# A two-layer attention and mixture-of-experts kernel: first context group loaded in four column pieces, setup block folded into the values stage

## The chip, the cores and the metric

The kernel runs on one core of one Trainium2 chip. The metric is device time of one execution in microseconds (us), lower is better. One execution is also taken by the hardware profiler; its rows are in microseconds from the first instruction of the span, unless marked ns. About 0.5% is what a measurement of this kernel can tell from no change.

## The reference

Inputs are `x` and `ctx_2048`, both 16 x 128 x 512 in float32 (16 batches of 128 rows), and the weights of four blocks, each added to `x`: an mLSTM attention whose keys and values are the context, a feed-forward block with 8 routed experts and a shared one, a cross attention of 16 heads with rms-normed queries and keys, and a linear layer with ternary weights. What matters here is the very first work of the program, which belongs to the third block but depends on the context alone:

```python
v_img = (img_ctx @ vi_w + vi_b).reshape(B, -1, H, D)     # 2048 x 512 times 512 x 2048
```

The context is also turned (rows to columns) for the keys and for the gates of the first block, so the same stage makes the turned context, its two-part split for the three-pass products, and the gates.

## The kernel before, in words

All work is written out per engine in blocks; each block ends with a barrier of all engines, and inside a block engines meet through semaphores only.

`setup` (line 158) is a block of its own, with work on GpSimd alone: four memsets (identity, two epsilons, ones), then an `affine_select` (L171) that makes the identity matrix for TensorE's transposes. Then comes `mlstm`, whose first block is the values stage, `values_and_gates` (line 185).

The values stage computes the values of one context tile of 128 rows (a "unit", 52 of them in all) times 512 weight columns (a "quad" of four heads). The contraction of 512 is cut in four chunks of 128. The context comes in four groups of four batches (1 MB each, `load_ctx`, L249), and a group and chunk together are one turn `t` = 4 x group + chunk:

- TensorE `turn(t)` (L585): four 128x128 transposes (L593) into one bank. For group 0 it waits for the whole group; from t = 4 on it waits as well until DVE and ACT have read the same bank, which is `trail_done` and `plain_done` at t - 3.
- ACT `turn_lead(t)` (L386) rounds the bank into `lead`; DVE `turn_trail(t)` (L480) writes bank minus lead into `trail`; ACT `turn_plain(t)` (L393) copies the bank once more and stores it to memory (L395).
- the weight's chunk c gets the same split: ACT `wl` (L406), DVE `wt` (L485).
- TensorE `first_chunk(c)` (L611): 12 products (three passes, four tiles) of chunk c for units 0 to 3, in banks 0 to 3. Later units (L597) do their 12 products in one go, each after ACT or DVE has emptied its bank (`keep_even` L400, `keep_odd` L534).

Each engine runs its list in the order written. ACT's opening order is lead 0, wl 0, lead 1, wl 1, lead 2, wl 2, lead 3, wl 3; plain 0 to 3; lead 4 to 7; plain 4, plain 5; keep_even 0, keep_even 2; plain 6, plain 7; then per unit. DVE's is trail 0, wt 0, ... trail 3, wt 3; trail 4 to 7; keep_odd 1 and 3; then per unit, among it the next weight's `wt` from unit 10 on and row statistics from unit 8 on. TensorE's is turns 0 to 3, first_chunk 0, turn 4, first_chunk 1, turn 5, first_chunk 2, turns 6 and 7, first_chunk 3; then for each unit from 4 on a turn (while there are any) and the unit.

SyncE's queue: group 0 (1 MB, rows of 2 KB), the four weight chunks (256 KB each, L260), group 1; after turn 3 group 2; after turn 7 group 3, the eight small loads of gate weights and biases (L269 to L273), the store of the first values (L283), two of x (L254) and the next weight quad of 1 MB (L290), which GpSimd splits (L370).

```python
            for t in range(C):
                turn(t)
            for c in range(C):
                first_chunk(c)
                if c < C - 1:
                    turn(C + c)
                if c == C - 2:
                    turn(C + c + 1)
```

Of the kernel before, what the change touches and what calls it, by code (L numbers as in the profile page):

```python
# [20 lines left out]
ALU = mybir.AluOpType  # L21
# [3 lines left out]
P = 128  # L25
B, S, D = 16, 128, 512
T = B * S
C = D // P
GB = 4
# [44 lines left out]
class Phase:  # L74
# [23 lines left out]
    def sb(self, name, shape, dt=F32):  # L98
        return self.stack.enter_context(self.nc.sbuf_tensor(f"{self.name}_{name}", shape, dt))

    def sem(self, name):
        self.sems.append(self.nc.alloc_semaphore(name=f"{self.name}_{name}"))
        return self.sems[-1]
# [51 lines left out]

def setup(nc, K):

    with Phase(nc, "setup") as ph:  # L160
        blank, made = ph.sem("blank"), ph.sem("made")
        block = ph.block()

        @block.gpsimd
        def _(pool):
            nc.gpsimd.memset(K.ident[:], 0.0).then_inc(blank, 1)
            nc.gpsimd.memset(K.eps5[:], 1e-5)
            nc.gpsimd.memset(K.eps6[:], 1e-6)
            nc.gpsimd.memset(K.ones[:], 1.0).then_inc(blank, 1)
            pool.wait_ge(blank, 2)  # L170
            nc.gpsimd.affine_select(out=K.ident[:], in_=K.ident[:], compare_op=ALU.not_equal, fill=1.0,  # L171
                                    base=0, pattern=[[-1, P]], channel_multiplier=1).then_inc(made, 1)
            pool.wait_ge(made, 1)

# [8 lines left out]
def values_and_gates(nc, K, M, A, E1, x_split, lead, trail, keep, a, v_dram, tail_dram, split_dram, xn_dram, ct_dram, g_dram):  # L185
    with Phase(nc, "values") as ph:
        sb, sem = ph.sb, ph.sem
# [13 lines left out]
        stage = [A.kT[:].rearrange("p c n -> p (c n)").rearrange("p (b d) -> p b d", b=GB), A.ctx[:]]  # L201
# [5 lines left out]
        out = [sb("out", [P, 4, GB, DH1]), A.out]  # L207
# [20 lines left out]
        turned, lead_done, trail_done, plain_done = sem("turned"), sem("lead_done"), sem("trail_done"), sem("plain_done")  # L228
        wl_done, wt_done = sem("wl_done"), sem("wt_done")
        product, even_done, odd_done = sem("product"), sem("even_done"), sem("odd_done")  # L230
        cleared, masks = sem("cleared"), sem("masks")
        wsum_done, wc_lead, wc_trail = sem("wsum_done"), sem("wc_lead"), sem("wc_trail")
        xn_done, x_turned, xT_done = sem("xn_done"), sem("x_turned"), sem("xT_done")
# [7 lines left out]
        block = ph.block()  # L241
        ps = K.ps

        def bank(t):
            return 4 + t % 4

        @block.sync
        def _(sp):
            def load_ctx(g):  # L249
                sp.dma_start(stage[g % 2], a["ctx_2048"][g * GB:(g + 1) * GB].rearrange("b s d -> s b d")  # L250
                             ).then_inc(ctx_loaded[g], 16)
# [3 lines left out]
                             ).then_inc(x_loaded[g], 16)  # L255

            w_dram = a["L1_xattn_vi_w"]
            load_ctx(0)
            for c in range(C):
                sp.dma_start(raw[:, c, :], w_dram[c * P:(c + 1) * P, 0:N]).then_inc(first_loaded[c], 16)  # L260
            load_ctx(1)
            sp.wait_ge(turned, C)
# [23 lines left out]
            for u in range(UNITS):  # L286
# [11 lines left out]
                if u in SPLITS:  # L298
                    g = SPLITS[u]
# [54 lines left out]
        @block.gpsimd  # L354
        def _(pool):
            own = Own(pool, own_pool)
            nc.gpsimd.memset(w_gate[:], 0.0)
            nc.gpsimd.memset(bias[:], 0.0).then_inc(cleared, 1)
            nc.gpsimd.memset(keep[:], 1.0)
            own(nc.gpsimd.memset(pen[:], 0.0))  # L360
            nc.gpsimd.memset(keep[:, :, 0:1], 0.0)
            nc.gpsimd.memset(pen[:, :, 0:1], -FAR).then_inc(masks, 1)
            for q in range(1, QUADS):
                pool.wait_ge(raw_loaded, 16 * q)
                if q > 1:
                    pool.wait_ge(product, OPENS[q - 1])
                if q == TAIL[0] + 2:
                    pool.wait_ge(tail_stored, 32)
                for c in range(C):
                    nc.gpsimd.tensor_scalar(wl[:, q % 2, c, :], raw[:, c, :], 1.0, None, ALU.mult).then_inc(wl_done, 1)  # L370
            Phase.clear_over(nc)
# [212 lines left out]
        def _(pe):  # L584
            def turn(t):  # L585
                g, c = divmod(t, C)
                if c == 0:
                    pe.wait_ge(ctx_loaded[g], 16)
                if t >= C:
                    pe.wait_ge(trail_done, t - C + 1)  # L590
                    pe.wait_ge(plain_done, t - C + 1)
                for b in range(GB):
                    ins = nc.tensor.transpose(ps[:, bank(t), b * S:(b + 1) * S], stage[g % 2][:, b, c * P:(c + 1) * P],  # L593
                                              K.ident[:])
                ins.then_inc(turned, 1)
# [68 lines left out]
                                                  row[:, b * S:(b + 1) * S], K.ident[0:32, 0:32])  # L664
                    ins.then_inc(nat_T, 1)

            for t in range(C):
                turn(t)
            for c in range(C):
                first_chunk(c)  # L670
                if c < C - 1:
                    turn(C + c)
                if c == C - 2:
                    turn(C + c + 1)
            for u in range(GB, UNITS):
                if u + C < G * C:
                    turn(u + C)
# [2607 lines left out]
def two_layers(nc, a, out):  # L3285
# [20 lines left out]
    with ExitStack() as stack:  # L3306
        kept = lambda name, shape: stack.enter_context(nc.sbuf_tensor(name, shape, F32))
        K = Kept()
# [8 lines left out]
        R.slot = stack.enter_context(nc.sbuf_tensor("slot", [P, 2, B], U32))  # L3317
        R.expert = stack.enter_context(nc.sbuf_tensor("expert", [P, TILES + 1], U32))
        K.stats, K.mv, K.rstd = kept("stats", [P, B, 6]), kept("mv", [P, B, 2]), kept("rstd", [P, B])
        setup(nc, K)  # L3320
        routed_weights = [a[f"L0_ffn_w_{n}"] for n in ("gate", "up", "down")]
        with Phase(nc, "of_ffn") as outer:
            with Phase(nc, "of_shared") as inner:
# [44 lines left out]
```

## Time and profile before

| | |
|---|---|
| runs | 1348.18, 1343.0, 1348.6 us; median 1348.18 |
| profiled execution | 1345.04 us, of it span 1343.3 us, granted TensorE clock 0.987 |
| busy share of the span | PE 95%, PEld 79%, DVE 63%, ACT 55%, POOL 28% |
| DMA | 277.06 MB, mean 206 GB/s |
| TensorE idle before its first transpose | 7.85 us |

PE is TensorE's matmuls and transposes, PEld its weight loads, DVE VectorE, ACT ScalarE, POOL GpSimd, SP SyncE; SPq and ACTq are their sequencers issuing DMAs. A row of the timeline gives the start, the duration, the engine, the line, the operation, output and inputs, and in brackets how long the engine had been idle before and what released it. Rows with xN merge N instructions that follow each other. Matmuls are pipelined, so the distance between two starts tells more than a duration.

### The profile page before, as it was taken

What the parts mean: (1) busy time and instruction counts of PE and PEld (TensorE: products, weight loads), DVE (VectorE), ACT (ScalarE), POOL (GpSimd) and SP (SyncE); (2) the same over time, 40 slices, a digit from 0 to 9 for tenths busy, and PEclk for the clock granted to TensorE, in tenths of its full rate; (3) what the DMA queues carried; (4) which work ended last, traced back from release to release, by engine and by line L of the source; (5) the groups of instructions that cost most, each with busy time, mean ns of one, the idle gap of its engine ahead of it and who ended that gap; (6) DMA issues with size and microseconds to landing.
All of it is one profiled execution on the core that took longest, in us unless ns stands there. A gap on an engine that the chain in (4) does not pass through costs nothing. (4 is left out here: it accounts for less than half of the span.)

```text
span 1343.3 us, 24403 instructions
## 1 busy us (share of the span) xinstructions
PE 1279.5 (95%) x7358; PEld 1059.4 (79%) x7359; DVE 841.2 (63%) x1613; ACT 741.6 (55%) x1831; POOL 379.5 (28%) x353
## 2 busy tenths in 40 slices
PE   7999997999999899899999989999989999999998
PEld 6787776777777778688877778878888888888986
DVE  3545546778779863644445477553577777777865
ACT  5225538787886431454455445445775655565561
POOL 0111014274737016399131342144010000000041
PEclk9999999999999899899999999999989999999999
DMA  7897399787864394666559776564475555555403
GB/s 255 290 365 255 139 317 322 268 265 253 280 223 166 88 345 174 223 180 208 148 170 314 255 261 189 158 210 172 143 213 166 160 157 167 159 162 157 120 28 126
DMA packets 166599, 277.06 MB, mean 206 GB/s; under 512 B 29744, under 2 KB 58160, under 8 KB 166256
## 3 DMA queue, kind: packets, MB, share of 16 engines
q1 hardware_dynamic: 140704, 220.50, 51.2%
q0 software_dynamic: 8672, 29.37, 6.7%
q10 hardware_dynamic: 17136, 26.09, 5.3%
q8 instruction: 47, 0.77, 0.2%
q14 instruction: 40, 0.33, 0.1%
HBM read 167.11 MB, written 108.80 MB: 205 GB/s over the span
## 5 line engine op out<-in xcount | busy, mean ns | idle before, releaser
L120 PE MATMUL banks<-of_shared_split,key_lead 128*128 128x512 f32 x256 | 104.7, 409 | 11.5 <-DVE key_trail L1403 10.1
L2984 ACT ACTIVATE prob<-banks,attend_row,rq 128x128 f32<-128x128 f32 x248 | 110.5, 470 | 0.0
L2997 ACT ACTIVATE attend_ol<-banks,of_attend_vbias 128x512 fp32r<-128x512 f32 x64 | 44.2, 691 | 117.0 <-PE banks L3196 117.0
L120 PE MATMUL banks<-wo,attend_ol 128*128 (+1 forms) x256 | 106.2, 415 | 0.0
L120 PE MATMUL banks<-queries_rows_split,queries_wl 128*128 128x512 f32 x256 | 100.8, 394 | 0.0
L122 PE MATMUL banks<-wo,attend_ot 128*128 (+1 forms) x256 | 100.7, 393 | 0.0
L122 PE MATMUL banks<-of_shared_split,key_trail 128*128 128x512 f32 x256 | 100.6, 393 | 0.0
L121 PE MATMUL banks<-of_shared_split,key_lead 128*128 128x512 f32 x256 | 100.1, 391 | 0.0
L121 PE MATMUL banks<-wo,attend_ol 128*128 (+1 forms) x256 | 99.9, 390 | 0.0
L122 PE MATMUL banks<-queries_rows_split,queries_wt 128*128 128x512 f32 x256 | 99.8, 390 | 0.0
L121 PE MATMUL banks<-queries_rows_split,queries_wl 128*128 128x512 f32 x256 | 99.7, 390 | 0.0
L2966 POOL TENSOR_TENSOR x_kept<-x_kept,attend_tern_bias 128x512 f32<-128x512 f32 x12 | 15.5, 1294 | 282.6 <-ACT of_attend_raw L3023 281.0
L2634 DVE TENSOR_TENSOR queries_total<-queries_total,queries_sq 128x512 f32<-128x512 f32 x60 | 45.0, 751 | 75.2 <-ACT queries_sq L2547 75.2
L2543 ACT ACTIVATE queries_head<-banks,queries_bias 128x512 f32<-128x512 f32 x64 | 44.1, 689 | 81.7 <-PE banks L122 76.1
L1013 ACT ACTIVATE heads_dec<-mlstm_gmax,mlstm_nat 128x128 f32<-128x128 f32 x256 | 81.3, 389 | 10.0 <-POOL mlstm_gmax L921 4.8
L120 PE MATMUL banks<-of_shared_split,of_ctx_lead 128*128 128x512 f32 x208 | 84.0, 404 | 2.0 <-DVE of_ctx_trail L480 1.8
L1198 DVE TENSOR_TENSOR heads_total<-heads_total,heads_ksq 128x512 f32<-128x512 f32 x60 | 56.6, 943 | 42.1 <-ACT heads_ksq L1055 41.8
L122 PE MATMUL banks<-of_shared_split,of_ctx_trail 128*128 128x512 f32 x208 | 82.3, 396 | 0.0
L3085 DVE TENSOR_TENSOR x_kept<-x_kept,banks 128x512 f32 (+1 forms) x64 | 44.0, 688 | 60.8 <-PE banks L122 60.2
L121 PE MATMUL banks<-of_shared_split,of_ctx_lead 128*128 128x512 f32 x208 | 81.7, 393 | 0.0
L3177 PEld LDWEIGHTS banks<-attend_kn,q_ahead 128*128 128x128 f32 x496 | 66.0, 195 | 6.2 <-issue 1.9
L120 PEld LDWEIGHTS banks<-of_shared_split,key_lead 128*128 128x128 f32 x256 | 48.1, 188 | 28.5 <-DVE key_trail L1403 14.9
(399 smaller groups left out, 3535.0 us busy)
## 6 DMA issues: line engine op xcount, KB each, us to landing
mlstm_gmax<-running_max SPq DMA_DIRECT2D x32, 512.0 KB, 6.2
k_heads<-heads_key ACTq DMA_DIRECT2D x64, 256.0 KB, 4.4
q_heads<-queries_head SPq DMA_DIRECT2D x64, 256.0 KB, 2.6
q_ahead<-q_heads SPq DMA_DIRECT2D x64, 256.0 KB, 4.2
of_attend_k<-k_heads SPq DMA_DIRECT2D x60, 256.0 KB, 4.1
of_attend_v<-v_heads SPq DMA_DIRECT2D x60, 256.0 KB, 3.2
key_raw<-in_L_xattn_ki_w SPq DMA_DIRECT2D x20, 512.0 KB, 5.5
sorted_rows<-of_shared_split SPq DMA_DIRECT2D x2, 5120.0 KB, 27.6
```

The costliest lines, as they stand in the source:

```text
L120: nc.tensor.matmul(out, lead_l, lead_r, start=first, stop=False)
L121: nc.tensor.matmul(out, lead_l, trail_r, start=False, stop=False)
L122: return nc.tensor.matmul(out, trail_l, lead_r, start=False, stop=last)
L1013: ins = nc.scalar.activation(dec[:, n % 2, b], gmax[:, h // 2 % 4, h % 2 * N + b * S:h % 2 * N + (b + 1) * S], ACT.Exp, scale=-1.0, bias=M ...
L1198: nc.vector.tensor_tensor(t, t, ksq[:, m % 2, :], ALU.add).then_inc(total_done, 1)
L2543: nc.scalar.activation(head[:, u % HEADS_RING, :], ps[:, u % 4, :], ACT.Identity, bias=bias[:, h:h + 1]).then_inc(head_done, 1)
L2634: nc.vector.tensor_tensor(t, t, sq[:, u % 2, :], ALU.add).then_inc(total_done, 1)
L2966: nc.gpsimd.tensor_tensor(K.x[:, b, :], K.x[:, b, :], tern_bias[:], ALU.add).then_inc(tern_bias_done, 1)
L2984: ins = nc.scalar.activation(prob[:, j % 2, b, :], ps[:, j % 2, b * S:(b + 1) * S], ACT.Exp, bias=row[:, j % 2, 1, b:b + 1], scale=rq[:, b ...
L2997: nc.scalar.activation(ol[:, par, j, :], ps[:, 4 + j % 2, :], ACT.Identity, bias=vbias[:, bass.ds(quad_of(it) * 4 + j, 1)]).then_inc(ol_do ...
L3085: nc.vector.tensor_tensor(xb, xb, ps[:, 6 + b % 2, :], ALU.add).then_inc(acc_done, 1)
L3177: ins = nc.tensor.matmul(ps[:, j % 2, s], q[:, j, s], kn[:, j % 2, s], start=True, stop=True)
```

## The change

The setup block goes; its instructions stand at the head of GpSimd's list in the values stage, with one semaphore (`made`) that TensorE waits for before its first transpose. Group 0 of the context is loaded in four pieces of 128 columns (256 KB each, runs of 512 bytes), each ahead of the weight chunk of the same number, with a semaphore each. TensorE's order becomes turns 0 and 1, first_chunk 0, turn 2, first_chunk 1, turn 3, first_chunk 2, turns 4 to 7, first_chunk 3. The lists of ACT and DVE stay as they are.

```diff
-def setup(nc, K):
-
-    with Phase(nc, "setup") as ph:
-        blank, made = ph.sem("blank"), ph.sem("made")
-        block = ph.block()
-
-        @block.gpsimd
-        def _(pool):
...
+def setup(nc, K, pool, blank, made):
+    nc.gpsimd.memset(K.ident[:], 0.0).then_inc(blank, 1)
+    nc.gpsimd.memset(K.ones[:], 1.0)
+    nc.gpsimd.memset(K.eps5[:], 1e-5)
+    nc.gpsimd.memset(K.eps6[:], 1e-6)
+    pool.wait_ge(blank, 1)
+    nc.gpsimd.affine_select(out=K.ident[:], in_=K.ident[:], compare_op=ALU.not_equal, fill=1.0,
+                            base=0, pattern=[[-1, P]], channel_multiplier=1).then_inc(made, 1)
...
             w_dram = a["L1_xattn_vi_w"]
-            load_ctx(0)
             for c in range(C):
+                sp.dma_start(stage[0][:, :, c * P:(c + 1) * P],
+                             a["ctx_2048"][0:GB, :, c * P:(c + 1) * P].rearrange("b s d -> s b d")).then_inc(ctx_first[c], 16)
                 sp.dma_start(raw[:, c, :], w_dram[c * P:(c + 1) * P, 0:N]).then_inc(first_loaded[c], 16)
             load_ctx(1)
...
         def _(pool):
             own = Own(pool, own_pool)
+            setup(nc, K, pool, blank, made)
             nc.gpsimd.memset(w_gate[:], 0.0)
...
                 g, c = divmod(t, C)
-                if c == 0:
+                if g == 0:
+                    pe.wait_ge(ctx_first[c], 16)
+                elif c == 0:
                     pe.wait_ge(ctx_loaded[g], 16)
...
-            for t in range(C):
-                turn(t)
+            pe.wait_ge(made, 1)
+            turn(0)
+            turn(1)
             for c in range(C):
                 first_chunk(c)
-                if c < C - 1:
-                    turn(C + c)
+                if c + 2 < C:
+                    turn(c + 2)
                 if c == C - 2:
-                    turn(C + c + 1)
+                    for t in range(C, 2 * C):
+                        turn(t)
...
-        setup(nc, K)
```

## Rows read from the trace of the kernel before

**Rows 1.** The page: busy time, share of the span, instructions of TensorE

```profile
PE 1279.5 (95%) x7358; PEld 1059.4 (79%) x7359; DVE 841.2 (63%) x1613; ACT 741.6 (55%) x1831; POOL 379.5 (28%) x353
```

**Rows 2.** Timeline of all engines from the start: start, duration, engine, line, operation

```profile
0.81 0.20 POOL L166 MEMSET ident<- 128x128 f32 x1 [0.29 <-POOLq L3359]
...
1.47 0.28 POOL L171 TENSOR_SCALAR_AFFINE_SELECT ident<-ident 128x128 f32<-128x128 f32 x1 [0.24 <-POOL ones L169]
2.22 0.45 SPq L250 DMA_DIRECT2D mlstm_kT<-in_ctx  x1
...
2.73 2.24 SPq L260 DMA_DIRECT2D mlstm_gmax<-in_L_xattn_vi_w  x4
...
7.85 3.66 PE L593 MATMUL banks<-ident,mlstm_kT 128*128 128x128 f32 x16 [7.85 <-DMA mlstm_kT<-in_ctx]
```

**Rows 3.** Windows of the opening: stretch, length, granted clock, DMA share, GB/s

```profile
3.80:4.20 0.40, 1.00 0.07 26
...
5.00:6.00 1.00, 1.00 1.03 401
```

**Rows 4.** DMA issues of the whole span: size of one, median us to landing

```profile
of_ffn_raw<-sorted_rows SPq DMA_DIRECT2D x39, 256.0 KB, 3.0
```

**Rows 5.** Timeline of DVE: split of the first weight chunk

```profile
10.24 0.68 DVE L485 TENSOR_TENSOR of_shared_split<-mlstm_gmax,of_shared_split 128x512 fp32r<-128x512 f32 x1
```

**Rows 6.** Timeline of TensorE alone: first chunks of units 0 to 3, unit 4

```profile
11.18 0.56 PE L120 MATMUL banks<-of_shared_split,of_ctx_lead 128*128 128x512 f32 x1
...
14.11 0.60 PE L593 MATMUL banks<-ident,mlstm_ctx 128*128 128x128 f32 x4
14.47 0.47 PE L120 MATMUL banks<-of_shared_split,of_ctx_lead 128*128 128x512 f32 x1
...
20.48 1.03 PE L593 MATMUL banks<-ident,mlstm_ctx 128*128 128x128 f32 x8
21.28 0.48 PE L120 MATMUL banks<-of_shared_split,of_ctx_lead 128*128 128x512 f32 x1
...
24.90 0.47 PE L120 MATMUL banks<-of_shared_split,of_ctx_lead 128*128 128x512 f32 x1 [0.17 <-ACT of_ffn_raw L400]
```

**Rows 7.** Timeline of ACT: leads, copies kept for the store, first eviction

```profile
9.00 0.60 ACT L386 ACTIVATE of_ctx_lead<-banks 128x512 fp32r<-128x512 f32 x1 [5.49 <-PE banks L593]
...
13.01 0.61 ACT L393 ACTIVATE mlstm_gmax<-banks 128x512 f32<-128x512 f32 x1
...
17.06 0.60 ACT L386 ACTIVATE of_ctx_lead<-banks 128x512 fp32r<-128x512 f32 x1 [0.40 <-ACT mlstm_gmax L393]
...
21.12 1.09 ACT L386 ACTIVATE of_ctx_lead<-banks 128x512 fp32r<-128x512 f32 x2 [2.59 <-PE banks L593]
22.09 0.61 ACT L393 ACTIVATE mlstm_gmax<-banks 128x512 f32<-128x512 f32 x1
...
24.16 1.08 ACT L400 ACTIVATE of_ffn_raw<-banks 128x512 f32<-128x512 f32 x2 [0.40 <-ACT mlstm_gmax L393]
```

**Rows 8.** Timeline of SyncE's queue: what follows turn 7

```profile
21.55 0.37 SPq L250 DMA_DIRECT2D mlstm_ctx<-in_ctx  x1
...
30.31 0.40 SPq L283 DMA_DIRECT2D v_heads<-of_ffn_raw  x1
...
33.92 1.05 SPq L290 DMA_DIRECT2D mlstm_gmax<-in_L_xattn_vi_w  x1
```

**Rows 9.** Timeline of all engines about unit 12

```profile
47.57 5.87 POOL L370 TENSOR_SCALAR of_shared_split<-mlstm_gmax 128x512 fp32r<-128x512 f32 x4 [43.48 <-DMA mlstm_gmax<-in_L_xattn_vi_w]
...
51.31 0.67 DVE L480 TENSOR_TENSOR of_ctx_trail<-banks,of_ctx_lead 128x512 fp32r<-128x512 f32 x1
...
52.04 0.58 PE L120 MATMUL banks<-of_shared_split,of_ctx_lead 128*128 128x512 f32 x1 [1.82 <-DVE of_ctx_trail L480]
...
55.79 0.39 PE L120 MATMUL banks<-of_shared_split,of_ctx_lead 128*128 128x512 f32 x1
```

**Rows 10.** Windows after that wait: PE busy, granted clock, DMA share, GB/s

```profile
54.00:56.00 2.00, 2.00 (x6) 0.57 1.05 406
```

More of the change, by code:

```diff
@@ L154, in root @@
                                   ).then_inc(self.rooted, 1)
-def setup(nc, K):
-    with Phase(nc, "setup") as ph:
-        blank, made = ph.sem("blank"), ph.sem("made")
-        block = ph.block()
-        @block.gpsimd
-        def _(pool):
[L166 to L173, printed above, removed]
+def setup(nc, K, pool, blank, made):
[6 more added lines that the diff above has]
+                            base=0, pattern=[[-1, P]], channel_multiplier=1).then_inc(made, 1)
 class Gates:
@@ L230, in values_and_gates @@
         product, even_done, odd_done = sem("product"), sem("even_done"), sem("odd_done")
+        blank, made = sem("blank"), sem("made")
+        ctx_first = [sem(f"ctx_first{c}") for c in range(C)]
         cleared, masks = sem("cleared"), sem("masks")
```

## The prediction

> **What bounds the kernel now.** I read the page first: TensorE is busy 95% of the span [rows 1], so a change can gain only where TensorE stands still or runs at its lower clock, and an earlier start is kept only if nothing further on gives it back. Then the timeline of the opening. GpSimd enters the setup block at 0.81, the identity is made at 1.47, SyncE issues the first load only at 2.22, and the first transpose starts at 7.85, released by that load [rows 2]. The first product follows at 11.18 [rows 6], with the split of the first weight chunk on DVE (10.24) just ahead of it [rows 5]. From there to unit 4 at 24.90 TensorE runs without a hole but for 0.17 us [rows 6]. The next hole is 1.82 us before unit 12 at 52.04 [rows 9]. Its chain: the next weight quad is issued at 33.92 [rows 8] and lands at 47.57; GpSimd splits its chunks; DVE, which takes its list in order, needs the first of them for a `wt`, then does statistics, and only then at 51.31 the trail that unit 12 needs [rows 9]. That load's place is set by SyncE: group 3 goes out at 21.55, after turn 7, then eight small loads until 30.31, then three of 1 MB and this one [rows 8]. After the hole the clock is low, 0.57 of full over 54 to 56 us [rows 10], which is the 1.2 GHz level for most of it.
>
> **The barrier.** Without the block SyncE issues at 0.81 instead of 2.22, the time at which GpSimd enters the first block against the second [rows 2]: 1.41 us earlier. GpSimd's five instructions now run beside the load. The identity is ready at about 1.8 (1.47 + 0.28), far ahead of any landing, so the new wait on `made` costs 0; if the cover were gone it would cost its 0.9 us. The memsets behind it on GpSimd move to about 1.8 and nobody waits for them before turn 7. ACT's table load also moves ahead.
>
> **The first piece.** No row shows a piece of 256 KB in runs of 512 bytes as the first load. From below: 256 KB lands in 3.0 us at the median [rows 4]. From above: the whole 1 MB took 5.63 us (2.22 to 7.85) [rows 2]. I build it: 1.98 us from issue to data (still 26 GB/s at 3.80 to 4.20, so data starts at 4.20), 0.26 MB at 401 GB/s is 0.66 us [rows 3], and a tail. The tail of the 1 MB load: 1.05 MB at the same rate is 2.62, so its data ends near 6.82 and the transpose starts 1.03 later. Sum 3.67 us; turn 0 at 4.48. Between turn 0 and the first product I keep 3.33 us (7.85 to 11.18), since ACT and DVE do the same four steps: first product at 7.81, **3.37 us earlier**. Bounds: 0.81 + 3.0 + 3.33 = 7.14 (4.04 earlier) and 0.81 + 5.63 + 3.33 = 9.77 (1.41 earlier). The issues: five DMAs took 2.22 to 4.97 [rows 2], 0.55 each, so nine end near 5.8; group 1 is issued some 0.7 us later than now (4 x 0.55 = 2.2 more, less 1.41) and is needed by turn 4 only at about 17. Weight chunk 0 goes out second and comes some 0.7 us after the piece, while ACT wants it 1.65 us after turn 0: hidden. Half the rate for the short runs would add 0.66, inside the bounds.
>
> The Trainium skill speaks against small pieces (DMA: Bandwidth & Descriptors, Rules for kernel authors: at least 1 MiB per DMA for full bandwidth) and gives a fixed cost of about 2.0 us per DMA; by an estimate from that page the piece would land after about 2.7 us and the first product would come 1.0 us earlier than in my sum. The traces' 3.0 us for 256 KB agrees only roughly.
>
> **The order on TensorE and ACT.** Here something is given back. Call the start of the first product F. First_chunk 0 takes 2.93 (11.18 to 14.11), a turn 0.36 (14.11 to 14.47), a later chunk 2.83 (from 14.47 to 20.48 are two and a turn) [rows 6]. Turn 3 now stands behind two chunks and turn 2: F + 6.12. ACT's lead 3 follows 0.64 later (20.48 to 21.12), wl 3 and plain 0 follow at 0.50 each (four pairs from 9.00 to 13.01), so plain 0 is at F + 7.76 and, four copies with their stores taking 4.05 (13.01 to 17.06), plain 3 at F + 10.80 and lead 4 at F + 11.81 [rows 7]. Turn 7 wants plain 3; from an ACT start to TensorE's go is 0.74 (24.16 to 24.90), so turn 7 starts at F + 11.54 and first_chunk 3 at F + 11.90. Now they start at F + 9.70 (20.48 + 0.40) and F + 10.10 (21.28): **1.84 and 1.80 us are given back**, 0.72 of it the two turns moved behind F, the rest waiting. And ACT is late for more: four leads from F + 11.81 on, 0.485 each (two in 0.97, 21.12 to 22.09), plain 4 at F + 13.75, keep_even 0 2.07 later (22.09 to 24.16) at F + 15.82, unit 4 at F + 16.56. Now it is F + 13.72: 2.84 given back, with a new hole of about 1.5 us before unit 4, since first_chunk 3 and turn 8 end at F + 11.90 + 2.83 + 0.36 = F + 15.09.
>
> **Unit 12.** SyncE's list from group 3 on follows turn 7, so the weight quad, and with it unit 12, moves by 3.37 - 1.84 = 1.53 us earlier. TensorE's own way there moves by only 3.37 - 2.84 = 0.53, so the hole shrinks from 1.82 to 0.82 and unit 12 still follows SyncE's chain. DMA is full there (406 GB/s at share 1.05 [rows 10]) and I take its bytes as unchanged.
>
> **The clock.** The 16 first transposes take 3.33 us, 0.21 each [rows 2, 6], eight later ones 0.80 us, 0.10 each [rows 6]: the first run at half speed, 1.2 GHz by this reading, though the granted clock reads 1.00 [rows 3], and the products at 11.18 already run fast. In the changed kernel only eight transposes, with a gap, come before first_chunk 0. What a slow stretch costs is at unit 12: nine products from 52.04 to 55.79 take 3.75 us [rows 9] against 9 x 0.236 = 2.12 at the pace above: 1.63 us. First_chunk 0 loses between 0 and 1.63; I take 1.63, as its row is the nearest, a product stretch after a hole. At unit 12 the other way: after a hole of 0.82 us instead of 1.82 the clock may hold, which gives 0 to 1.63 back; I take 1.63, as the nearer row is the 0.17 us hole at 24.90 with no fall behind it. The Trainium skill (TensorE: Matmul & The Clock Gate, Part 1) says that the default state is throttled and that activity releases it; by that the first product starts slow, as in my sum, and without it the sum would be 1.63 better.
>
> **The sum.** 3.37 - 1.84 - 1.63 + 1.63 = 1.53 us faster, 1343.5 on the profiled execution's 1345.04. That execution lies 3.1 us under the median of 1348.18, and the runs spread over 5.6 us; the mean of all four times is 1346.2, and I take the forecast from there: **1344.7 us**. Best bound 4.04 - 1.84 + 1.63 = 3.8 faster; worst 1.41 - 1.84 - 1.63 = 2.1 slower, where unit 12's clock falls as now.
>
> **Rivals.**
> - The opening's gain arrives whole. If copies on ACT are not the brake that I count (1.84 more), or first_chunk 0 runs fast (1.63 more), or both, 3.2 to 5.0 us are gained: about 1342. For it: rows 6 show TensorE nearly without holes. Against it: turn 7 does wait for plain 3 in the code, and ACT's start times are read, not guessed.
> - Slower: ACT's lateness wins. The mechanism is the wait of turn 7 for plain 3, 1.84 us, plus the slow first_chunk 0, 1.63 us, against the earlier start. It decides from the point where turn 0 starts later than 4.38 us (3.47 lost against 3.47 won) and no clock is regained at unit 12; at 6.44 it ends 2.1 us slower: 1348.3. For it: my 4.48 sits right at that point. Against it: the smaller hole at unit 12. By the same page of the skill the new hole before unit 4 could also lower the clock, another 1.63 there; this eats the hole at unit 12 and changes the end by about 1.
> - The change does not do what it says: SyncE still starts at 2.22, as entering the block costs the same. Then 3.37 - 1.41 - 1.84 = 0.12 gained: 1346.1.
> - Something outside the first 60 us moves by several us, by the scatter that the runs show.
>
> **How the numbers follow.** Forecast 0.50, gain whole 0.22, slower 0.17, no earlier start 0.05, outside 0.06. The range takes both bounds from 1346.2 (1342.4 and 1348.3) and half the spread, 2.8: 1339.6 to 1351. Half a per cent, which is what a measurement here can tell, is 6.7 us; no case but the last reaches that alone, the second with favourable scatter. So faster by over 0.5% 0.08, within 0.89, slower 0.03.
>
> **What would show it.** SyncE's first issue at 0.8, first transpose at 4.5, first product at 7.8 with its chunk taking 4.6 instead of 2.93; TensorE idle before turns 6 and 7 with ACT L393 as the releaser, and about 1.5 us before unit 4, which starts at 7.81 + 16.56 + 1.63 = 26.0, released by ACT L400; unit 12 at 52.04 - 1.53 + 1.63 = 52.1, with a hole under 1 us and the clock up after it. I am wrong in mechanism if turn 7 does not wait for ACT, or if the first product is not earlier by at least 1.4 us; wrong in size if the whole moves by over 6.7 us.

## The result and the profile after

The changed kernel takes **1350.91 us** (median of 20 runs, 1345.29 to 1359.12), the kernel before, run on the same chip, 1346.22 us (20 runs, 1341.01 to 1351.64). The ratio is 1.0033, 95% interval 1.0017 to 1.0048: slower by 4.7 us. That lies inside the half per cent that counts as no change and just inside the stated range, but on the other side from the 1.5 us gain that I forecast.

The profiled execution took 1347.16 us (span 1345.4). On the page TensorE's share still reads 95%, so this line says nothing about a change of a third of a per cent:

```profile
PE 1283.9 (95%) x7358; PEld 1062.1 (79%) x7359; DVE 839.6 (62%) x1613; ACT 742.0 (55%) x1831; POOL 376.9 (28%) x353
```

SyncE's queue, from its timeline (start, duration, engine, line, operation), beside [rows 2, 8]:

```profile
0.81 0.45 SPq L253 DMA_DIRECT2D mlstm_kT<-in_ctx  x1
1.32 0.49 SPq L255 DMA_DIRECT2D mlstm_gmax<-in_L_xattn_vi_w  x1
...
4.93 0.43 SPq L244 DMA_DIRECT2D mlstm_ctx<-in_ctx  x1
16.27 0.38 SPq L244 DMA_DIRECT2D mlstm_kT<-in_ctx  x1
21.72 0.37 SPq L244 DMA_DIRECT2D mlstm_ctx<-in_ctx  x1
22.13 2.18 SPq L264 DMA_DIRECT2D values_w_gate<-in_L_xattn_Wi  x3
24.35 4.96 SPq L264 DMA_DIRECT2D values_w_gate<-in_L_xattn_Wf  x3
29.35 1.43 SPq L267 DMA_DIRECT2D values_bias<-in_L_xattn_bi  x1
...
33.65 1.11 SPq L285 DMA_DIRECT2D mlstm_gmax<-in_L_xattn_vi_w  x1
```

The first issue is at 0.81 as forecast. The line to look at is the one at 16.27: the load of context group 2, which waits for turn 3. My prediction speaks of groups 1 and 3 and never of this one.

TensorE's timeline, against [rows 2, 6]; in brackets the idle time before an instruction and what ended it:

```profile
3.96 1.08 PE L591 MATMUL banks<-ident,mlstm_kT 128*128 128x128 f32 x4 [3.96 <-DMA mlstm_kT<-in_ctx]
6.22 1.12 PE L591 MATMUL banks<-ident,mlstm_kT 128*128 128x128 f32 x4 [1.18 <-DMA mlstm_kT<-in_ctx]
7.14 0.76 PE L120 MATMUL banks<-of_shared_split,of_ctx_lead 128*128 128x512 f32 x1
7.71 0.63 PE L121 MATMUL banks<-of_shared_split,of_ctx_lead 128*128 128x512 f32 x1
8.13 0.63 PE L122 MATMUL banks<-of_shared_split,of_ctx_trail 128*128 128x512 f32 x1
...
12.40 0.64 PE L591 MATMUL banks<-ident,mlstm_kT 128*128 128x128 f32 x4
...
15.64 0.60 PE L591 MATMUL banks<-ident,mlstm_kT 128*128 128x128 f32 x4
...
20.06 0.63 PE L591 MATMUL banks<-ident,mlstm_ctx 128*128 128x128 f32 x4 [0.18 <-ACT mlstm_gmax L389]
21.06 0.63 PE L591 MATMUL banks<-ident,mlstm_ctx 128*128 128x128 f32 x4 [0.37 <-ACT mlstm_gmax L389]
...
26.07 0.47 PE L120 MATMUL banks<-of_shared_split,of_ctx_lead 128*128 128x512 f32 x1 [1.20 <-ACT of_ffn_raw L396]
```

The first product comes 4.04 us earlier than before (7.14 against 11.18), but its chunk takes 5.26 us (7.14 to 12.40) instead of 2.93, because the products start 0.43 apart instead of 0.23 in this profile. Turn 3 is at 15.64. Turns 6 and 7 wait for ACT's copies, unit 4 waits for its eviction, and so unit 4 starts 1.17 us *later* than before. ACT itself, in its timeline, stands idle for 4.58 and 2.09 us before leads 2 and 3; that is where the copies of turns 0 to 2 would have had room:

```profile
13.07 0.60 ACT L382 ACTIVATE of_ctx_lead<-banks 128x512 fp32r<-128x512 f32 x1 [4.58 <-PE banks L591]
...
16.28 0.60 ACT L382 ACTIVATE of_ctx_lead<-banks 128x512 fp32r<-128x512 f32 x1 [2.09 <-PE banks L591]
...
17.29 0.59 ACT L389 ACTIVATE mlstm_gmax<-banks 128x512 f32<-128x512 f32 x1
```

Windows of the kernel before (stretch, length, busy time and count on PE, PEld, DVE, ACT, POOL, then granted clock, DMA share, GB/s):

```profile
12.00:18.00 6.00, 6.00 (x32) 4.95 (x32) 2.83 (x6) 4.08 (x9) 0.00 (x0) 1.00 0.97 367
18.00:24.00 6.00, 6.00 (x32) 5.04 (x31) 2.96 (x5) 2.71 (x5) 0.00 (x0) 1.00 0.26 82
```

and of the changed one:

```profile
12.00:18.00 6.00, 6.00 (x31) 4.89 (x30) 2.38 (x4) 2.72 (x5) 0.00 (x0) 1.00 0.06 19
18.00:24.00 6.00, 5.45 (x32) 4.41 (x31) 2.25 (x5) 4.35 (x8) 0.00 (x0) 1.00 0.99 331
```

Before, the DMA engines work from 12 to 18 us (2.2 MB) and rest from 18 to 24 (0.5 MB), so the list that follows turn 7 finds them free. Now it is the reverse: 0.1 MB, then 2.0 MB. Group 2 (out at 16.27 instead of 11.54) and the four stores of the turned context (from 17.91 on instead of 13.65) have slid into the stretch in which group 3 and the eight small loads go out.

In this execution that did no harm yet. The weight quad lands at 47.24 (47.57 before), and unit 12 starts at 51.71 with a short hole and the granted clock stays at 1.00, as forecast [rows 9, 10]; timeline of all engines:

```profile
47.24 5.88 POOL L366 TENSOR_SCALAR of_shared_split<-mlstm_gmax 128x512 fp32r<-128x512 f32 x4 [43.86 <-DMA mlstm_gmax<-in_L_xattn_vi_w]
...
51.71 0.50 PE L120 MATMUL banks<-of_shared_split,of_ctx_lead 128*128 128x512 f32 x1 [0.31 <-DVE of_ctx_trail L476]
```

It is also one of the quicker executions of the changed kernel, 3.75 us under the median, so one trace can't settle this case; further profiles of both kernels stand below.

### The profile page after: what moved, and what is told of

The parts are those of the page before. It is cut to its first block and busy times, and to the rows that moved or that the text cites. A ratio compares the mean times of both kernels' runs of the same rounds, so it can differ in the third digit from the quotient of the medians.

```text
span 1345.4 us, 24387 instructions
## 1 busy us (share of the span) xinstructions
PE 1283.9 (95%) x7358; PEld 1062.1 (79%) x7359; DVE 839.6 (62%) x1613; ACT 742.0 (55%) x1831; POOL 376.9 (28%) x353
## 5 line engine op out<-in xcount | busy, mean ns | idle before, releaser
L120 PE MATMUL banks<-of_shared_split,key_lead 128*128 128x512 f32 x256 | 106.2, 415 | 8.8 <-DVE key_trail L1403 8.4
L121 PE MATMUL banks<-of_shared_split,key_lead 128*128 128x512 f32 x256 | 102.1, 399 | 0.0
```

Source lines behind the costliest of these rows:

```text
L120: nc.tensor.matmul(out, lead_l, lead_r, start=first, stop=False)
L121: nc.tensor.matmul(out, lead_l, trail_r, start=False, stop=False)
```

## The experiments

The expectations are quoted as they were written before each run, and they name theories. Theory A: the difference is chance, from stretches at the lower clock that fall now here, now there. Theory B: the pieces or the new order on TensorE bring the loss. Theory C: losing the barrier brings it. Theory D, which grew out of the first four runs: the new order sends group 2 out late, and the list behind it makes the next weight quad late. Ratios are to the kernel before, measured on the same chip, with 95% intervals.

**The parts by themselves.** `e1_barrier_only` folds the constants into the stage and keeps the whole load and the old order:

```
-        setup(nc, K)
...
+            setup(nc, K, pool, blank, made)
...
+            pe.wait_ge(made, 1)
```

> Setup block folded into the values stage, loads and TensorE order as before. Theory A (the opening is worth what it shows and the 4.7 us come from extra stretches at the lower clock between 190 and 320 us that either kernel can get by chance): TensorE's stream is 1.4 us ahead from the first transpose to 448 us, the number of low-clock stretches before 448 us varies from one to three, the time is within 2 us of before. Theory B (the pieces or the new order on TensorE bring the loss): 1.4 us faster, with one low-clock stretch before 448 us as before. Theory C (losing the barrier brings it, by what it does to later stages): 3 us or more slower.

Measured: 1347.64 us, ratio 1.0010 [0.9987, 1.0033]. First transpose at 6.42 instead of 7.85, first product at 9.71, group 2 out at 10.09, quad landed at 46.90, unit 12 at 51.37. The barrier's 1.4 us arrive at TensorE, half of them is left at unit 12, and the end shows no gain.

`e2_pieces_only` is the changed kernel with the block of its own put back (the reverse of that diff).

> Four pieces and the new TensorE order, setup block kept. Everything of the opening as in the changed kernel but 1.4 us later: first transpose at 5.4, hole before unit 4 of 1.2 us, TensorE 0.6 us ahead of before at 60 us. Theory A: time within 2 us of before. Theory B: slower than before by 4 to 6 us. Theory C: within 1 us of before.

Measured: 1349.47 us, 1.0029 [1.0012, 1.0046]. A loss is there without the barrier's removal, so the pieces or the order bring one; at 3.0 us it is smaller than the 4 to 6 expected. Group 2 goes out at 16.75, the quad lands at 51.62.

`e3_act_fill` uses ACT's idle time before leads 2 and 3:

```
-            for t in range(C):
-                turn_plain(t)
+                if c == 1:
+                    turn_plain(0)
+                    turn_plain(1)
+                if c == 2:
+                    turn_plain(2)
+            turn_plain(3)
```

> The changed kernel, with ACT's copies plain 0 and 1 moved ahead of lead 2 and plain 2 ahead of lead 3, into the 4.6 us in which ACT stands idle. The holes before turns 6 and 7 (0.18 and 0.37) and before unit 4 (1.20) go; if TensorE's way to unit 12 were the limit the gain would be 1.7, but unit 12 hangs on the load that SyncE issues after turn 7, which comes 0.6 to 0.9 us earlier, so that much is gained and a hole of up to 1.5 us stands before unit 12 again. Theory A: between 1 faster and 2 slower than the changed kernel by chance of the clock. Theory that the delay on ACT is what costs the 4.7 us: back to before or faster.

Measured: 1349.36 us, 1.0024 [1.0005, 1.0043]. The holes before turns 6 and 7 are gone and the one before unit 4 shrinks to 0.3 us, yet the time is still lost. Its quad lands at 46.31, earlier than in any profile of the kernel before. Waiting for ACT is real, but taking it away does not win the time back.

**The same kernels again**, without an edit: `e4_changed_again`, `e13_changed_third`, `e14_changed_fourth`, `e18_changed_same_chip`, and of before `e5_before_again`, `e15_before_third`.

> The changed kernel once more, for a second profile of it. Theory A: the opening to 60 us is the same within 0.3 us, the low-clock stretches between 60 and 448 us stand at other places or in another number, and the time is 3 to 6 us over before again if the loss is real. If the stretches stand at the same three places (193, 224, 309) they belong to the kernel, not to chance.

> The kernel before, once more, for a second profile of it. Theory D (turn 3 is late in the changed kernel, so group 2 and the four stores of the turned context go out 4.3 to 4.7 us later and run into group 3 and the eight small loads; the queue behind them, with the next weight quad, lands late and unit 12 waits): the next weight quad is split by GpSimd from 47.6 again, within 0.5 us, unit 12 starts at 52.0. Theory A (chance of the clock): unit 12 moves by some us from profile to profile in this kernel too.

> A third profile of the changed kernel. If the loss sits before unit 12 (theory D), unit 12 starts later than 52.0 in most profiles of it: 51.7 and 56.7 so far, so 53 to 57 here. If it sits elsewhere (theory A), 51.5 to 52.

> A fourth profile, same expectations: theory D 53 to 57 for the start of unit 12, theory A 51.5 to 52.

> A third profile of the kernel before. Theory D: unit 12 at 52 to 53 again (52.04 and 52.9 so far), the issue of the small loads over at 30 to 31.3. Theory A: as far spread as the changed kernel's.

> The changed kernel beside it on the same chip, for the comparison: 1350 to 1351, unit 12 between 51.7 and 56.7.

The changed kernel came out at 1350.88 us, 1.0027 [1.0002, 1.0052], and 1349.38 us, 1.0015 [0.9998, 1.0032] (e18), with single executions of 1346.33 and 1349.49 (e13, e14); before at 1346.99, 1.0001 [0.9978, 1.0024], and a single 1346.95 (e15). The difference repeats, though it is smaller and not clear of noise in e18. Their profiles show where they part (the last column is the DMA share over 32 to 34 us):

| profile | group 3 out | small loads through | quad landed | from group 3 | unit 12 | hole before it | DMA share |
|---|---|---|---|---|---|---|---|
| before | 21.55 | 30.20 | 47.57 | 26.0 | 52.04 | 1.8 | 1.05 |
| before, e5 | 21.89 | 31.20 | 48.13 | 26.2 | 52.60 | 2.0 | 0.97 |
| before, e15 | 21.90 | 30.49 | 48.08 | 26.2 | 52.55 | 2.0 | 1.07 |
| changed | 21.72 | 31.25 | 47.24 | 25.5 | 51.71 | 0.3 | 0.95 |
| changed, e18 | 21.54 | 30.95 | 47.05 | 25.5 | 51.52 | 0.3 | 1.06 |
| changed, e14 | 21.40 | 32.45 | 49.08 | 27.7 | 53.55 | 2.5 | 0.51 |
| changed, e13 | 21.50 | 32.35 | 49.53 | 28.0 | 54.00 | 2.8 | 0.63 |
| changed, e4 | 21.27 | 33.06 | 50.63 | 29.4 | 55.09 | 4.1 | 0.31 |

The kernel before needs 26.0 to 26.2 us from group 3's issue to the quad's landing every time. The changed one needs 25.5 to 29.4, and within its five profiles the landing is late where SyncE was late in getting through the small loads: up to 31.3 it lands at about 47, past 32.3 at 49 and later. In the late ones, and only there, the DMA engines are partly idle over 32 to 34 us. Its latest profile, e4, in the timelines of SyncE, GpSimd and TensorE:

```profile
15.82 0.38 SPq L244 DMA_DIRECT2D mlstm_kT<-in_ctx  x1
21.27 0.37 SPq L244 DMA_DIRECT2D mlstm_ctx<-in_ctx  x1
21.68 2.36 SPq L264 DMA_DIRECT2D values_w_gate<-in_L_xattn_Wi  x3
24.08 5.62 SPq L264 DMA_DIRECT2D values_w_gate<-in_L_xattn_Wf  x3
29.75 2.82 SPq L267 DMA_DIRECT2D values_bias<-in_L_xattn_bi  x1
...
35.33 1.45 SPq L285 DMA_DIRECT2D mlstm_gmax<-in_L_xattn_vi_w  x1
...
50.63 1.50 POOL L366 TENSOR_SCALAR of_shared_split<-mlstm_gmax 128x512 fp32r<-128x512 f32 x1 [47.24 <-DMA mlstm_gmax<-in_L_xattn_vi_w]
...
55.09 0.50 PE L120 MATMUL banks<-of_shared_split,of_ctx_lead 128*128 128x512 f32 x1 [4.08 <-DVE of_ctx_trail L476]
```

and its windows:

```profile
12.00:18.00 6.00, 6.00 (x32) 5.03 (x31) 2.58 (x4) 2.86 (x6) 0.00 (x0) 1.00 0.24 46
...
32.00:34.00 2.00, 2.00 (x12) 1.65 (x11) 1.08 (x2) 0.96 (x2) 0.00 (x0) 1.00 0.31 87
```

against the kernel before:

```profile
32.00:34.00 2.00, 2.00 (x10) 1.63 (x10) 0.69 (x1) 0.67 (x2) 0.00 (x0) 1.00 1.05 382
```

A load of one bias takes SyncE 2.82 us to issue. The small loads hold SyncE until 33.06, and the DMA engines run dry while it is held and just after: share 0.31 over 32 to 34 us, where before has 1.05. The big loads that should feed them stand behind the small ones. e2, e16 and e17, whose quads land late as well, show such a gap too: 0.61 over 32 to 34 in e2, 0.39 over 30 to 31 in e16, 0.50 over 34 to 36 in e17. Why one bias load can hold SyncE so long no run shows.

**Moving loads only.** The opening on TensorE and ACT is the changed kernel's in both of these. `e6_changed_small_early` puts the small loads behind group 1:

```
             load_ctx(1)
-            sp.wait_ge(turned, C)
-            load_ctx(2)
-            sp.wait_ge(turned, 2 * C)
-            load_ctx(3)
             sp.wait_ge(cleared, 1)
...
+            sp.wait_ge(turned, C)
+            load_ctx(2)
+            sp.wait_ge(turned, 2 * C)
+            load_ctx(3)
```

> The changed kernel with the eight small loads issued right after group 1, where DMA stands idle from 12 to 16 us, instead of after group 3. Theory D: SyncE issues the next weight quad at 27 to 30 instead of 33.7 to 35.3, it lands by 44 instead of 47.2 to 50.6, no hole before unit 12 and no low clock at 52 to 56; 4 to 6 us faster than the changed kernel (1345 to 1347), and faster than before by 0 to 2 us. Theory A: no change against the changed kernel beyond 2 us.

Measured: 1346.36 us, 0.9985 [0.9967, 1.0003]. The time came as theory D had it, the quad did not: it lands at 47.10, not by 44, although its load goes out at 29.03 instead of 33.65.

`e8_changed_group2_pieces` leaves them and sends group 2 out column by column, as each turn frees its columns:

```
-            sp.wait_ge(turned, C)
-            load_ctx(2)
+            for c in range(C):
+                sp.wait_ge(turned, c + 1)
+                sp.dma_start(stage[0][:, :, c * P:(c + 1) * P],
+                             a["ctx_2048"][2 * GB:3 * GB, :, c * P:(c + 1) * P].rearrange("b s d -> s b d")).then_inc(ctx_loaded[2], 16)
...
```

> The changed kernel with group 2 loaded in four column pieces too, each as soon as the turn that frees its columns is done: two pieces go out at about 7 and 8, one at 13, one at 16, instead of the whole at 16. Theory D: half of its 1 MB leaves the crowded stretch after 16 us, some 1.3 us of full DMA, so the next weight quad lands 1 to 1.5 us earlier and the time is 1 to 2 us under the changed kernel. Theory A: same as the changed kernel.

Measured: 1345.15 us, 0.9991 [0.9973, 1.0009]. The windows show the gap before 18 us half filled and the DMA engines busy over 32 to 34 us (e8; share 1.01 over 32 to 34 in e6):

```profile
12.00:18.00 6.00, 6.00 (x31) 4.89 (x30) 2.39 (x4) 2.73 (x5) 0.00 (x0) 1.00 0.55 153
...
32.00:34.00 2.00, 2.00 (x13) 1.66 (x12) 0.96 (x3) 1.20 (x2) 0.00 (x0) 1.00 1.03 349
```

Two edits that touch nothing but when loads go out win back the loss, more than the 1 to 2 us expected of e8. Both intervals lie below 1.0017, where that of the changed kernel's 20 runs begins; they overlap that of e18. With the three measurements of the changed kernel taken together (44 runs) and those of e6 and e8 (24 runs), each run divided by the mean of the kernel before on its chip, the difference is 4.4 us, 95% interval 2.5 to 6.4. The first chunk is as slow in them as in the changed kernel (7.18 to 12.43 in e8). But e8's quad lands at 47.17, and so neither profile has it earlier than the two early profiles of the changed kernel (47.24 and 47.05). With one profile each, that the edits prevent the late landings is likely and not shown.

**Order or pieces.** `e10_changed_old_order` has the pieces with the old order on TensorE:

```
-            turn(0)
-            turn(1)
+            for t in range(C):
+                turn(t)
             for c in range(C):
                 first_chunk(c)
-                if c + 2 < C:
-                    turn(c + 2)
+                if c < C - 1:
+                    turn(C + c)
...
```

> No barrier and four pieces, but TensorE's old order, turns 0 to 3 first. Theory D (turn 3's delay is the cause, not the pieces): group 2 goes out at 9 to 10, its transfer is over before group 3's, the small loads end at about 29, and the time is that of the barrier alone, 1346 to 1348, so 3 us under the changed kernel. Rival (the 256 KB pieces in 512-byte runs cost it): as slow as the changed kernel, 1350 to 1351.

`e17_barrier_new_order` has the whole load with the new order, still without the barrier:

```
+            load_ctx(0)
             for c in range(C):
-                sp.dma_start(stage[0][:, :, c * P:(c + 1) * P],
-                             a["ctx_2048"][0:GB, :, c * P:(c + 1) * P].rearrange("b s d -> s b d")).then_inc(ctx_first[c], 16)
...
```

> The missing corner: barrier removed, group 0 loaded whole, TensorE's new order. First product at about 9.7, turn 3 at about 16 to 18, group 2 out then. If the order alone carries the loss: 1350 to 1351, as the changed kernel. If pieces and order each carry a part: 1348.5 to 1350. If the loss needs the pieces: 1347 to 1348, as with the barrier alone.

| medians and ratios, all without the barrier | old order | new order |
|---|---|---|
| whole load | 1347.64, 1.0010 (e1) | 1350.59, 1.0022 (e17) |
| four pieces | 1349.24, 1.0022 (e10) | 1350.91, 1.0033; 1350.88, 1.0027 (e4); 1349.38, 1.0015 (e18) |

The new order loses time without the pieces: e17 is at 1.0022 [1.0005, 1.0039]. That doesn't make it the sole cause. The pieces with the old order have the same ratio, e10's expectation of 1346 to 1348 was missed, and the step from e1 to e17 is 2.3 us with an interval of -0.6 to 5.2, each run again divided by the mean of the kernel before on its chip. The four cells don't divide the loss between order and pieces. e17's windows show the idle DMA engines at their clearest:

```profile
12.00:18.00 6.00, 6.00 (x29) 4.88 (x29) 1.29 (x2) 1.31 (x3) 0.00 (x0) 1.00 0.00 0
```

Its group 2 goes out at 17.80, the quad lands at 51.54 and unit 12 starts at 56.00. In e10 (1.0022 [0.9999, 1.0044]) all four turns come first, and the fourth piece is there only at 9.82, where the whole load let the first turn go at 6.42:

```profile
3.87 1.08 PE L591 MATMUL banks<-ident,mlstm_kT 128*128 128x128 f32 x4 [3.87 <-DMA mlstm_kT<-in_ctx]
6.69 1.12 PE L591 MATMUL banks<-ident,mlstm_kT 128*128 128x128 f32 x4 [1.73 <-DMA mlstm_kT<-in_ctx]
8.24 1.12 PE L591 MATMUL banks<-ident,mlstm_kT 128*128 128x128 f32 x4 [0.43 <-DMA mlstm_kT<-in_ctx]
9.82 1.12 PE L591 MATMUL banks<-ident,mlstm_kT 128*128 128x128 f32 x4 [0.46 <-DMA mlstm_kT<-in_ctx]
```

**The slow first chunk.** `e16_changed_warm` adds 14 transposes of the identity, into a bank that holds nothing yet, while TensorE waits for pieces:

```
             pe.wait_ge(made, 1)
+            busy(9)
             turn(0)
+            busy(5)
             turn(1)
```

> The changed kernel with idle-time transposes of the identity on TensorE (nine before turn 0, five before turn 1, into a bank that turn 3 overwrites), so that the clock is up when the first product comes. First_chunk 0 takes 3.0 us instead of 5.26, so turn 3, group 2, turn 7 and all behind them come 2.2 us earlier. Theory D with the low clock as a part of it: 2 to 4 us under the changed kernel, 1347 to 1349. If the low clock has no part: same as the changed kernel.

Measured: 1350.74 us, 1.0032 [1.0011, 1.0054]. TensorE's timeline:

```profile
1.60 2.18 PE L667 MATMUL banks<-ident 128*128 128x128 f32 x9 [1.60 <-POOL ident L164]
...
4.57 0.71 PE L667 MATMUL banks<-ident 128*128 128x128 f32 x5
...
7.26 0.48 PE L120 MATMUL banks<-of_shared_split,of_ctx_lead 128*128 128x512 f32 x1
7.58 0.40 PE L121 MATMUL banks<-of_shared_split,of_ctx_lead 128*128 128x512 f32 x1
...
10.46 0.48 PE L120 MATMUL banks<-of_shared_split,of_ctx_lead 128*128 128x512 f32 x1
```

First_chunk 0 now takes 2.85 us and a turn, 3.20 in all, and everything behind it moves 2.3 us up: group 3 goes out at 19.39. But the quad lands at 49.50, 30.1 us after it, and unit 12 starts at 53.96 with a hole of 4.91 us. A lead of 2.3 us in the opening turned whole into waiting in this profile. Running the first chunk fast does not win the loss back; what it would be worth with the quad in its old place no run shows.

**Late group 2 by itself.** `e11_before_group2_late` is the kernel before with `sp.wait_ge(turned, C)` ahead of group 2 turned into `sp.wait_ge(turned, 6)`.

> The kernel before with nothing changed but the wait ahead of group 2: it goes out after turn 5, at about 18, instead of after turn 3, at 11.5. The suspected cost alone, a little over its size. Theory D: its transfer runs into group 3 and the small loads, the small loads' issue ends at 32 to 34 instead of 30.2, the next weight quad lands at 49 to 51 instead of 47.6, and the time is 2 to 4 us over before. Theory A: same as before within 1 us.

Measured: 1345.35 us, 0.9982 [0.9959, 1.0005]. Group 2 goes out at 18.72, the quad lands at 49.02 and unit 12 starts at 53.49, about 1 us later than before. The time did not follow. The DMA engines have no gap over 32 to 34 us here (share 1.01). So group 2 going out late does not bring the loss by itself: this run speaks against the simplest form of my explanation.

**Towards a better version.** `e7_before_small_early` is before with the edit of e6; `e12_barrier_small_early` is e1 with it; `e9_all_moves` is the changed kernel with the edits of e3 and e8 and the small loads between group 2's second and third piece.

> The kernel before with the same move of the eight small loads. The hole of 1.82 us before unit 12 and the slow stretch after it (1.63 us) go: 3.4 us faster than before, if nothing later gives it back, about 1343. Theory A says the same of this run; it prices the hole.

> The kernel before with the barrier removed and the small loads right after group 1, no pieces and the old order. It shows whether pieces and new order have any part in the best version. Theory D: hole before unit 12 gone, 3 to 5 us faster than before: 1342 to 1344.

> The changed kernel with three repairs together: group 2 in column pieces, each behind the turn that frees it; the eight small loads between its second and third piece; ACT's copies in ACT's idle stretch. Theory D: no hole before turns 6 and 7, none over 0.3 before unit 4, the next weight quad issued by 28 and landed by 46; TensorE 3 to 4 us ahead of before at 60 us and no low clock at 50 to 56; 3 to 6 us faster than before at the median, 1341 to 1344, and 2 to 3 faster than either repair alone. Theory A: as the repairs alone.

Measured: e7 1343.19 us, 0.9983 [0.9959, 1.0008]; e12 **1341.99 us, 0.9966 [0.9942, 0.9989]**; e9 1345.02 us, 0.9972 [0.9951, 0.9992]. The lowest median is that of the simplest: no barrier, whole load, old order, small loads early. It beats both kernels clear of noise; against e7 and e9 the intervals overlap. e9 missed its 1341 to 1344, and the repairs together are not shown to be better than either alone. e12's queue on SyncE and the landing on GpSimd:

```profile
7.03 6.01 SPq L258 DMA_DIRECT2D values_w_gate<-in_L_xattn_Wf  x3
...
14.19 0.42 SPq L243 DMA_DIRECT2D mlstm_kT<-in_ctx  x1
20.56 0.39 SPq L243 DMA_DIRECT2D mlstm_ctx<-in_ctx  x1
...
26.63 4.40 SPq L283 DMA_DIRECT2D mlstm_gmax<-in_L_xattn_vi_w  x1
...
44.08 5.88 POOL L364 TENSOR_SCALAR of_shared_split<-mlstm_gmax 128x512 fp32r<-128x512 f32 x4 [40.70 <-DMA mlstm_gmax<-in_L_xattn_vi_w]
```

The small loads go out while TensorE is busy with group 0, the quad lands 3.5 us earlier than before, and unit 12 starts at 49.07 with no hole.

## Why the prediction was wrong

**The barrier: right.** SyncE at 0.81; the wait on `made` costs nothing.

**The first piece: mechanism right, size off.** Turn 0 at 3.96 against 4.48. The piece took 3.15 us from issue (0.81 to 3.96), close to my lower bound of 3.0 and not the 3.67 that I built. Turn 0 to the first product took 3.18 against the 3.33 kept. First product 4.04 us earlier, as in my best bound. By the fixed cost of about 2.0 us that the Trainium skill gives (DMA: Bandwidth & Descriptors, Anatomy of one DMA, where it is fitted to loads issued from GpSimd, not from SyncE as here) the estimate was 2.7 us; the measured 3.15 lies between that and mine. The pieces' issues were also cheaper than I took them: group 1 went out at 4.93, not 0.7 us later than its 5.01 of before.

**The slow first chunk: right, and the size about right.** 5.26 us in the first profile against the 4.6 that I named; in the other four it takes 4.83 to 5.02. Before isn't constant either: 2.93, 3.35 and 3.52 us in its three profiles. By the means (4.96 and 3.27) the loss is 1.7 us; I had 1.63. That it runs at half speed after an idle stretch and at full speed after extra transposes (0.43 against 0.23 between products) agrees with the rule that I cited from the Trainium skill (TensorE: Matmul & The Clock Gate, Part 1), that the default is throttled and activity releases it.

**What the new order gives back: right.** Turn 7 waits for ACT L389 and unit 4 starts at 26.07, forecast 26.0, released by the eviction, as I said it would be. Group 3 goes out at 21.27 to 21.72 in the five profiles; my steps give 21.55 - 1.53 + 1.63 = 21.65. Up to here the sum held within 0.4 us, in part by luck: in the first profile the first product is 0.67 us earlier than forecast and its chunk 0.7 us longer, and the two cancel at unit 4.

**Unit 12: here it failed.** The step was: "SyncE's list from group 3 on follows turn 7, so the weight quad, and with it unit 12, moves by 3.37 - 1.84 = 1.53 us earlier", with "DMA is full there [...] and I take its bytes as unchanged". From group 3 to the quad I kept the 26.0 us of the one profile. The five profiles show 25.5, 25.5, 27.7, 28.0 and 29.4, on average 1.2 us more. Unit 12 starts at 53.2 on average, where the kernel before has 52.0 to 52.6 and I forecast 52.1. I had asked what the new order does to group 1, and not to group 2, whose load waits for turn 3, the very turn that the change moves behind two chunks. It went out at 16.27 instead of 11.5, and the stores of the turned context, which follow ACT's late copies, came with it. Over 18 to 24 us, where SyncE's small loads and group 3 are due, the DMA engines move 2.0 MB where it was 0.5. The Trainium skill says it in a sentence (DMA: Bandwidth & Descriptors, Issuing engines are not separate DMA queues): DMAs of ScalarE and SyncE interleave on the same 16 engines whichever engine started them. The windows agree, with 0.06 before 18 us and 0.99 behind it. That page adds that the time to issue a DMA is usually small beside the DMA; here it isn't: eight small loads take 9.0 to 11.4 us of SyncE in the changed kernel, 8.2 to 8.9 in the one before, and in e4 the DMA engines run dry behind them. The 1.2 us of this step are a fifth of the 6.2 us between the forecast gain of 1.5 and the measured loss of 4.7. For the rest the failed step is the last one of the sum, that what unit 12 has reaches the end unchanged: in the first profile TensorE is 1.9 us ahead of before at 60 us and 2.1 us behind at the end, and what takes these 4.0 us is open. Scatter has a part in them: e15 and e5, the further profiles of before, fall back against the first one over the same stretch too, by 1.3 and 7.4 us.

**The clock regained: mostly right, not by the condition that I gave.** The granted clock falls to half behind unit 12 in all three profiles of before and in one of five of the changed kernel (e4, 55.8 us). But I tied it to a short hole, and in e13 and e14 it stays up behind holes of 2.8 and 2.5 us, where before falls behind 1.8 to 2.0.

**The slower rival**, which I gave 0.17, ended 2.1 us slower at worst through turn 7's wait for ACT. Turn 0 came at 3.96, on the good side of its point of 4.38, and e3 takes that wait away without winning the time back. The change ended on its side and not by its mechanism.

**What is shown and what is not.** Shown: the changed kernel is slower than before, and moving loads alone takes that away (e6, e8). A loss is also there with the barrier kept (e2) and with the new order without the pieces (e17). Taking away the low clock of the first chunk (e16) or the waits for ACT (e3) doesn't win the time back. Not shown: how the loss divides between the order and the pieces, and that the late quad is the way by which it reaches the end.

For the late quad speaks this: I took the same product, the one that starts near 60 us in the kernel before, in all twenty profiles. Its shift goes with the span of the same execution (correlation 0.84) and, averaged by kernel over 14 kernels, with the kernel's median (0.77, 0.8 us of time per us of shift). The ten profiles of the kernels that lose stand at +1.0 us there on average and at +5.5 near the end; those of the ten that don't at -1.4 and +2.0. So 2.4 of the 3.5 us between the groups are there by 60 us; most of the rest comes between 700 and 780 us, and I have no explanation for it.

Against it speak three things. Two kernels don't fit: e11 is 1.4 us late there and loses nothing, e3 is 1.3 us early and loses. The quads of e6 and e8 land no earlier than the changed kernel's early ones. And the loss is not in the profiles at hand: the changed kernel's five stand at -0.1 us at 60 us and took 1347.6 us on average, 3.3 under its median, while the three of before took 1348.3. The mean granted clock over the changed kernel's 20 runs is 0.984, against 0.985 to 0.986 in five other measurements of the kernel before; 0.001 of 1345 us is about 1.3 us of time (an estimate), and why the clock would be lower is open. Open too is why e16's quad took 30.1 us, and which part of e10's loss is the late fourth piece.

## What to carry to other kernels

When an instruction moves later on one engine, list every semaphore that it raises and every DMA that waits for one, not just the obvious one; a load that goes out 5 us later can find another load in its place. Look whether small loads of many short runs stand ahead of a big load that something waits for, and try them in a stretch where the DMA engines have room: here that was worth 0.34% together with the barrier's removal, while a first product 4 us earlier brought no gain. And a lead won ahead of a wait that a load ends is not kept unless that load moves too. The first profiles of the two kernels show the quad landing earlier in the changed one, the average of all shows it later; a difference of a third of a per cent needs repeated runs and repeated profiles.

## What the runs showed that I had not expected

- The same program lands the same load at different times: the quad at 47.05 to 50.63 in five profiles of the changed kernel, at 47.57 to 48.13 in three of before.
- The time that SyncE takes to issue one small load varies several times over: for the first bias 0.51 to 1.86 us in the three profiles of before, 1.20 to 2.82 in the five of the changed kernel, 0.59 in e12.
- The windows show a granted clock of 1.00 from the start although transposes and products run at half their later pace there; only the spacing of the instructions tells (0.43 against 0.23 us). The trace's own clock record begins later, with a step to full: at 11.4 us in before, 12.5 in the changed kernel and 4.5 in e16, and the windows show 1.00 for what lies ahead of it. The first product at the faster pace starts between 0.2 us ahead of that step and 0.7 us behind it in every profile but e16, where the step comes ahead of all products.
- Four pieces of 256 KB in runs of 512 bytes, with weight chunks between them, let the turns start at 3.87, 6.69, 8.24 and 9.82 (e10): the last comes 3.4 us after the whole megabyte would have been there (6.42).
